# GpSimd applies the first norm's weight and bias to x; the projection weights are split as they are

## The chip, the cores and the metric

One core of one Trainium2 chip runs the kernel. The metric is device time in microseconds (us); times of before are the median of three runs. Lower is better.

## The reference

Two attention layers run one after the other over 32 sequences of 128 tokens with 512 features, all in float32. What matters here, with one layer's names (layer 0 has 16 heads and ordinary softmax attention, layer 1 has 8 heads and linear attention with one softmax over the head's features for q and one over the tokens for k):

```python
xn = layer_norm(x) * norm_w + norm_b          # first norm, over 512 features
q, k, v = xn @ q_w + q_b, xn @ k_w + k_b, (xn @ v_w + v_b) * mask
y = attention(q, k, v)
e = silu(cond) @ emb_w + emb_b; scale, shift = split(e)
h = (layer_norm(y) * w2 + b2) * (1 + scale) + shift      # second norm
x = x + silu(h) @ out_w + out_b
```

## The kernel before

**Stages.** Sequences go in pairs (GROUP = 2); G = 16 pairs per layer, so there are 32 pair-steps in all, 0 to 15 for layer 0 and 16 to 31 for layer 1. In one step three pairs are in work at once: `k` (attention, second norm and output), `f` = the next pair (projections q, k, v) and `n` = the one after (load, first norm, transposition to `xt`). `late` is the second sequence of the pair before `k`, whose output is finished in this step. Sequences of a pair are slots b = 0 and 1. The step of pair 15 is `step_mixed`: attention of layer 0 beside projections of layer 1. Steps 0, 13, 14, 15, 16 and the last three are written out; the others run in two loops.

**Engines.** Each engine has its own list of work in a fixed order, written by hand in `start`, `step0`, `step_mixed` and `step1`, and waits on semaphores. No planner moves anything. All DMAs are issued by SyncE (SP), in order.
- TensorE (PE): each projection is computed as three float32r products, high times high, low times high and high times low (`three`, L1276 to L1278). Transpositions of xn (`turn`, L1272) and of yn (`turn_yn`, L1368) are matmuls with the identity.
- VectorE (DVE): moments of the norms (L880, L884), low parts (`w_lo` L835, `xt_lo` L893, `s_lo` L954), softmax pieces, `film_scale` (L941), silu (L948), output (L960).
- ScalarE (ACT): exponentials, tanh (L632), high parts (`w_hi` L570 and L572, `xt_hi` L584, `s_hi` L637), copies out of PSUM.
- GpSimd (POOL): finishes both norms. `rsqrt_norm` does three one-column operations (L454, L455, L457) and one over 128x512 (L462), which reads x_in and writes xn in `norm1`, or reads y_s and writes yn in `norm2`. It also adds the output bias to the residual (`residual`, L493), masks v (`v_mask`, L478 and L482) and adds the shift (`add_shift`, L488, writes z_s).

**GpSimd's order in a step of layer 1** (`step1`): norm1(n,0), residual(k,0), norm2(k,0), norm1(n,1), v_mask(f,0), norm2(k,1), add_shift(k,0), add_shift(k,1), v_mask(f,1), residual(k,1). In layer 0 (`step0`): norm1(n,0), residual(k,0), norm1(n,1), norm2(k,0), residual(k,1), v_mask(f,0), add_shift(k,0), norm2(k,1), v_mask(f,1), add_shift(k,1).

**TensorE's order in a step of layer 1**, from the middle on: query(k,0) (L1417), the first half of the values, query(k,1), queries1(f,0), turn_yn(k,0), values(f,1), turn_yn(k,1), queries1(f,1), turn(n,0), output(k,0), turn(n,1), then of the next step the transpositions of k and q, output(late,1), keys and again query.

**The norm's weight and bias before.** The first norm's w is folded into the weights: `high_part` and `low_part` scale each weight chunk by a column of w (`col[:, l, NW]`) as they split it. The norm's bias is folded into the projections' biases: for each of six weights (`TURN` lists them) `bias_part` (L1231, eight matmuls) multiplies norm_b with the raw weight into four row groups, ScalarE copies the result out (`bias_part_out`, L580), `bias_sum` (L1242 or L1245) adds the groups up on TensorE, and VectorE adds the sum to the bias (`bias_col` L844, `bias_wide` L849). Three of the six stand in `start`, one in step 13, one in step 14 and one in `step_mixed`.

```python
a = raw[l][j][c // 2][:, c % 2]
act.activation(hi[l][j][:, c], a, ACT.Identity, scale=col[:, l, NW, c:c + 1])
```

Of the kernel before, what the change touches and what calls it, by code (L numbers as in the profile page):

```python
# [7 lines left out]
BF16 = mybir.dt.bfloat16  # L8
# [47 lines left out]
def build(nc, t, out):  # L56
# [27 lines left out]
    with ExitStack() as ctx:  # L84
# [6 lines left out]
        def chunks(ap):  # L91
# [16 lines left out]
        col = sb("col", [P, 2, 6, C])  # L108
        NW, NBI, W2, B2, QB, KB = range(6)
        wide = sb("bias_wide", [P, 5, D])  # L110
        VALUE_BIAS, OUT_BIAS, QUERY_BIAS = (0, 3), (1, 4), 2
        film_ab = sb("film_ab", [P, 2, 2, C, B])
        silu_cond = film_ab[:, 1].rearrange("p i c b -> p (i c b)").rearrange("p (k b) -> p k b", k=KE)
        mask_parts = sb("mask_parts", [B, 3, P], BF16)
# [6 lines left out]
        ones_32nd = sb("ones_32nd", [P, P])  # L121
        norm_b_32 = sb("norm_b_32", [P, C, 32])
# [13 lines left out]
        y_t = sb("y_t", [P, D])  # L136
        y_s = sb("y_s", [P, D])
# [63 lines left out]
        PARS = (16 * 8, 16 * 6)  # L201
# [4 lines left out]
        spread, bias_pe, bias_act, bias_sum_pe, bias_dve = (  # L206
            sem(n) for n in ("spread", "bias_pe", "bias_act", "bias_sum_pe", "bias_dve"))
        TURN = {(0, WQ): 1, (0, WK): 2, (0, WV): 3, (1, WK): 4, (1, WV): 5, (1, WQ): 6}
        bias_part_at = [None, spare, y_t, spare, spare, spare, spare]
# [11 lines left out]
        s = stages("stats aggr rstd_a rstd_b neg_mean xn_full xn_turned xt_high xt_low "  # L221
# [56 lines left out]
        def _(sp):  # L278
# [10 lines left out]
            def load_wide(l, j, row):  # L289
                sp.dma_start(wide[:, row, :], layers[l]["b"][j].rearrange("(o n) -> o n", o=1).broadcast_to([P, D])  # L290
                             ).then_inc(par_in[l], 16)
# [41 lines left out]
            def start():  # L333
# [4 lines left out]
                load_wide(0, WV, VALUE_BIAS[0])  # L338
                load_col(0, QB, WQ, par_in[0])
# [5 lines left out]
                load_col(0, KB, WK, par_in[0])  # L345
                load_wide(0, WO, OUT_BIAS[0])
# [5 lines left out]
                for j in (WQ, WK):  # L352
                    sp.wait_ge(bias_pe, TURN[0, j])
                    sp.wait_ge(w_split[0][j], 1)
                    load_emb(0, (4 + 2 * j, 5 + 2 * j))
# [7 lines left out]
                load_wide(1, WQ, QUERY_BIAS)  # L363
                load_wide(1, WV, VALUE_BIAS[1])
                load_wide(1, WO, OUT_BIAS[1])
# [5 lines left out]
                sp.wait_ge(bias_sum_pe, 3)  # L371
                load_emb_bias(1, eb1_in)

            def step0(i, n, f, k, late, slot):
# [21 lines left out]
                if i == G - 2:  # L396
                    sp.wait_ge(bias_pe, TURN[1, WK])
                    sp.wait_ge(w_split[1][WK], 1)
                    load_weight(1, WQ)

            def step_mixed(i, n, f, k, late, slot):
                load_front(1, n)
                load_back(0, k, 0)
                store(0, late, 1)
                load_back(0, k, 1)
                sp.wait_ge(*done(s["pv"], LAST0))
                load_weight(1, WO)
                store(0, k, 0)
# [26 lines left out]
        def _(pool):  # L435
# [5 lines left out]
            pool.memset(ones_32nd[:], 1.0 / 32).then_inc(once, 1)  # L441
            pool.memset(ones_parts[:], 0.0).then_inc(once, 1)
            pool.wait_ge(once, 5)
# [3 lines left out]
            pool.wait_ge(once, 6)  # L447
            pool.tensor_tensor(pick[:], ident[:, 0:2 * B], ident[:, 2 * B:4 * B], ALU.add).then_inc(consts, 1)

            def rsqrt_norm(b, which, mv, a_in, rs, nm, full, src_ap, dst_ap, at, dst_free):  # L450
# [11 lines left out]
                pool.tensor_scalar(dst_ap, src_ap, v[:, 10:11], v[:, 9:10], ALU.add, ALU.mult  # L462
                                   ).then_inc(s[full].sem, 1)

            def norm1(n, b):
                pool.wait_ge(*landed(s["x_in_full"], n, b))
                rsqrt_norm(b, 0, "aggr", "rstd_a", "rstd_b", "neg_mean", "xn_full",
                           x_in[:, b, :], xn[:, b, :], n + b, "xn_turned")

            def norm2(k, b):  # L470
                rsqrt_norm(b, 1, "aggr2", "rstd2_a", "rstd2_b", "neg_mean2", "yn_full",
                           y_s[:], yn[:, b, :], k + b, "h_pe")
# [23 lines left out]
            def start():  # L496
                for b in range(GROUP):
                    norm1(pair(0), b)
                pool.memset(mask_wide[:], 0.0).then_inc(wide_clear, 1)
                for b in range(GROUP):  # L500
                    norm1(pair(1), b)
# [4 lines left out]
            def step0(i, n, f, k, late, slot):  # L506
                norm1(n, 0)
# [3 lines left out]
                norm1(n, 1)  # L511
# [15 lines left out]
            def step1(i, n, f, k, late, slot):  # L527
                if n:
                    norm1(n, 0)
                if i == G:  # L530
                    pool.wait_ge(par_in[1], PARS[1])
                    pool.wait_ge(film_dve, 6)
# [3 lines left out]
                if n:  # L536
                    norm1(n, 1)
# [21 lines left out]
        def _(act):  # L559
            act.wait_ge(consts, 1)  # L560

            def high_part(l, j, some=range(C)):
                act.wait_ge(w_in[l][j], 32)
                act.wait_ge(norm_in[l], 16 * 2)
# [10 lines left out]
            def bias_part_out(l, j, b):  # L575
                n = TURN[l, j]
                act.wait_ge(bias_pe, n)
                if n > 2:
                    act.wait_ge(bias_sum_pe, n - 2 if n == 3 else n - 1)
                act.activation(bias_part_at[n][:], bank[b][:], ACT.Copy).then_inc(bias_act, 1)  # L580
# [82 lines left out]
            def start():  # L663
# [5 lines left out]
                bias_part_out(0, WQ, 2)  # L669
                high_part(0, WK)  # L670
                act.wait_ge(bias_dve, 1)
                q_out(f, 0, 0)
                bias_part_out(0, WK, 3)
# [4 lines left out]
                bias_part_out(0, WV, 2)  # L678
                high_part(0, WO)
                act.wait_ge(bias_dve, 2)  # L680
# [5 lines left out]
            def step0(i, n, f, k, late, slot):  # L686
# [18 lines left out]
                if i == G - 3:  # L705
                    bias_part_out(1, WK, 6)
# [7 lines left out]
                if i == G - 2:  # L714
                    bias_part_out(1, WV, 6)
# [12 lines left out]
            def step_mixed(i, n, f, k, late, slot):  # L728
# [4 lines left out]
                act.wait_ge(bias_dve, TURN[1, WK])  # L733
# [10 lines left out]
                bias_part_out(1, WQ, 1)  # L744
# [60 lines left out]
        def _(dve):  # L805
            dve.wait_ge(consts, 1)

            def spread_norm_b(l):
                dve.wait_ge(norm_in[l], 16 * 2)
                dve.tensor_copy(norm_b_32[:], col[:, l, NBI, :].rearrange("p (c o) -> p c o", o=1).broadcast_to([P, C, 32])  # L810
                                ).then_inc(spread, 1)

# [27 lines left out]

            def bias_col(l, j, i, b):
                dve.wait_ge(par_in[l], PARS[l])
                dve.wait_ge(bias_sum_pe, TURN[l, j])
                dve.tensor_tensor(col[:, l, i, :], col[:, l, i, :], bank[b][:, 0:C], ALU.add).then_inc(bias_dve, 1)  # L844

            def bias_wide(l, j, row, b):
                dve.wait_ge(par_in[l], PARS[l])
                dve.wait_ge(bias_sum_pe, TURN[l, j])
                dve.tensor_tensor(wide[:, row, :], wide[:, row, :], bank[b][:], ALU.add).then_inc(bias_dve, 1)  # L849
# [162 lines left out]
            def start():  # L1012
# [3 lines left out]
                spread_norm_b(0)  # L1016
# [5 lines left out]
                bias_col(0, WQ, QB, 5)  # L1022
# [7 lines left out]
                bias_col(0, WK, KB, 5)  # L1030
# [6 lines left out]
                bias_wide(0, WV, VALUE_BIAS[0], 5)  # L1037
                dve.wait_ge(bias_dve, TURN[0, WV])
# [7 lines left out]
            def step0(i, n, f, k, late, slot):  # L1046
                if late:
                    film_scale(0, late + (-1), 1)
                if i == G - 3:
                    spread_norm_b(1)  # L1050
# [23 lines left out]
                if i == G - 3:  # L1074
                    bias_col(1, WK, KB, 6)
# [6 lines left out]
                if i == G - 2:  # L1082
                    bias_wide(1, WV, VALUE_BIAS[1], 3)
# [12 lines left out]
            def step_mixed(i, n, f, k, late, slot):  # L1096
# [16 lines left out]
                dve.wait_ge(bias_dve, TURN[1, WV])  # L1113
# [9 lines left out]
                bias_wide(1, WQ, QUERY_BIAS, 4)  # L1123
                dve.wait_ge(bias_dve, TURN[1, WQ])
# [78 lines left out]
        def _(pe):  # L1203
# [20 lines left out]

            def bias_part(l, j, b):

                claim(b, times(bias_act, TURN[l, j]))
                pe.wait_ge(spread, l + 1)
                pe.wait_ge(w_in[l][j], 32)
                for c in range(C):  # L1230
                    last = pe.matmul(bank[b][32 * c:32 * (c + 1), :], norm_b_32[:, c, :], raw[l][j][c // 2][:, c % 2],  # L1231
                                     start=True, stop=True, tile_position=(0, 32 * c))
                last.then_inc(bias_pe, 1)

            def bias_sum(l, j, b, as_column):
                n = TURN[l, j]
                claim(b, times(bias_dve, n))
                pe.wait_ge(bias_act, n)
                part = bias_part_at[n]
                if as_column:  # L1240
                    for c in range(C):
                        last = pe.matmul(bank[b][:, c:c + 1], part[:, c * P:(c + 1) * P], ones_32nd[:, 0:1],  # L1242
                                         start=True, stop=True)
                else:
# [355 lines left out]
```

## Time and profile before

| | |
|---|---|
| median of 3 runs | 1098.57 us (1097.37 to 1098.67) |
| the profiled execution's own time | 1097.78 us |
| its span, first to last instruction | 1096.0 us |
| mean granted TensorE clock | 0.993 |
| TensorE matmul busy | 1054.8 us, 96% |
| VectorE, ScalarE, GpSimd busy | 759.8, 591.6, 448.6 us |

The profile is of one execution. Busy time is that of instructions, without waits; matmuls overlap, so a busy TensorE need not be at its peak. The granted clock is the share of full speed, 2.4 GHz, that TensorE had; 0.5 is 1.2 GHz.

### The profile page before, as it was taken

Reading aid. Unit: us, or ns where it says so; the run is one execution under the profiler, and the core shown is the slowest. Engines: PE = TensorE matmul, PEld = TensorE weight load, DVE = VectorE, ACT = ScalarE, POOL = GpSimd, SP = SyncE. Lnnn points to the kernel's source line nnn. Section 1 sums busy time; section 2 is a strip of 40 time slices with the busy share of each in tenths; the row PEclk is TensorE's granted clock in tenths of the full one; section 3 lists DMA queues with packets and bytes.
Section 4 is the critical chain, followed back from the end, with each engine's and each line's share of the span. In section 5 each row is a group of like instructions: output and inputs, shape, how many; then the busy total and the mean of one; then the engine's idle time right before and its main releaser. Section 6 shows DMA issues by size and latency. Waiting matters only on the chain. (4 is left out here: it accounts for less than half of the span.)

```text
span 1096.0 us, 25953 instructions
## 1 busy us (share of the span) xinstructions
PE 1054.8 (96%) x8696; PEld 909.8 (83%) x8696; DVE 759.8 (69%) x1326; ACT 591.6 (54%) x1960; POOL 448.6 (41%) x783
## 2 busy tenths in 40 slices
PE   6999999999999999999999999999999999999995
PEld 4878888888888888888887778888888888888884
DVE  4656766676666766667678787777777777777764
ACT  5366667776677766776588443433343443434431
POOL 3242434334343343433343344444444444444432
PEclk9999999999999999999999999999999999999997
DMA  8824110111101111011102211111111111111011
GB/s 275 256 84 141 42 61 24 62 62 41 60 24 62 62 41 59 25 62 63 43 23 98 95 50 33 40 55 57 57 57 57 57 57 57 52 52 39 31 38 58
DMA packets 46017, 71.65 MB, mean 65 GB/s; under 512 B 10256, under 2 KB 14448, under 8 KB 45968
## 3 DMA queue, kind: packets, MB, share of 16 engines
q1 hardware_dynamic: 45968, 71.02, 20.3%
q8 instruction: 27, 0.44, 0.2%
q14 instruction: 22, 0.18, 0.1%
HBM read 54.19 MB, written 16.79 MB: 65 GB/s over the span
## 5 line engine op out<-in xcount | busy, mean ns | idle before, releaser
L1276 PE MATMUL bank<-xt_hi,w_hi 128*128 128x256 f32 x768 | 228.4, 297 | 3.1 <-DVE xt_lo L893 3.1
L1277 PE MATMUL bank<-xt_lo,w_hi 128*128 128x256 f32 x768 | 218.5, 284 | 0.0
L1278 PE MATMUL bank<-xt_hi,w_lo 128*128 128x256 f32 x768 | 218.3, 284 | 0.0
L454 POOL TENSOR_SCALAR stat<-stat 128x1 f32<-128x1 f32 x128 | 34.5, 270 | 441.8 <-DVE stat L884 417.7
L613 ACT ACTIVATE prob<-prob,neg_max 128x128 f32<-128x128 f32 x512 | 198.7, 396 | 6.7 <-DVE neg_max L907 6.6
L632 ACT ACTIVATE th<-z_s 128x512 f32<-128x512 f32 x64 | 40.5, 633 | 249.9 <-POOL z_s L488 249.8
L1276 PE MATMUL bank<-w_hi,xt_hi 128*128 128x512 f32 x384 | 158.3, 412 | 1.0 <-DVE w_lo L835 1.0
L1276 PEld LDWEIGHTS bank<-xt_hi,w_hi 128*128 128x128 f32 x768 | 148.9, 194 | 9.1 <-DVE w_lo L835 4.8
L1278 PE MATMUL bank<-w_hi,xt_lo 128*128 128x512 f32 x384 | 150.5, 392 | 0.0
L1277 PE MATMUL bank<-w_lo,xt_hi 128*128 128x512 f32 x384 | 149.8, 390 | 0.0
L1277 PEld LDWEIGHTS bank<-xt_lo,w_hi 128*128 128x128 f32 x768 | 148.6, 193 | 0.0
L1278 PEld LDWEIGHTS bank<-xt_hi,w_lo 128*128 128x128 f32 x768 | 148.2, 193 | 0.0
L1276 PE MATMUL bank<-w_hi,s_hi 128*128 128x512 f32 x256 | 106.7, 417 | 7.2 <-DVE s_lo L954 5.1
L488 POOL TENSOR_TENSOR z_s<-z_a,film_ab 128x512 f32<-128x512 f32 x64 | 68.5, 1071 | 107.2 <-DVE z_a L941 103.3
L1278 PE MATMUL bank<-w_hi,s_lo 128*128 128x512 f32 x256 | 101.1, 395 | 0.0
L1277 PE MATMUL bank<-w_lo,s_hi 128*128 128x512 f32 x256 | 100.5, 393 | 0.0
L613 ACT ACTIVATION_READ_ACCUMULATOR prob<-prob,neg_max 128x1 f32 x512 | 99.7, 195 | 0.0
L904 DVE TENSOR_TENSOR prob<-bank,mask_row 128x512 f32<-128x512 f32 x128 | 87.6, 684 | 12.7 <-PE bank L1327 12.1
L493 POOL TENSOR_TENSOR x_res<-x_res,bias_wide 128x512 f32<-128x512 f32 x64 | 88.7, 1386 | 16.2 <-DMA x_res<-between_layers 16.2
L621 ACT ACTIVATE room<-bank 128x512 f32<-128x512 f32 x128 | 74.4, 593 | 31.5 <-PE bank L1338 29.6
L907 DVE TENSOR_REDUCE neg_max<-prob 128x4 f32<-128x512 f32 x128 | 87.9, 687 | 4.4
L948 DVE SCALAR_TENSOR_TENSOR th<-th,z_s 128x512 f32<-128x512 f32 x64 | 47.2, 737 | 62.4 <-ACT th L632 61.4
(130 smaller groups left out, 2203.3 us busy)
## 6 DMA issues: line engine op xcount, KB each, us to landing
x_in<-in_x_dram SPq DMA_DIRECT2D x32, 256.0 KB, 2.8
x_res<-in_x_dram SPq DMA_DIRECT2D x32, 256.0 KB, 2.9
between_layers<-x_res SPq DMA_DIRECT2D x32, 256.0 KB, 2.0
x_in<-between_layers SPq DMA_DIRECT2D x32, 256.0 KB, 2.8
x_res<-between_layers SPq DMA_DIRECT2D x32, 256.0 KB, 2.8
out_dram<-x_res SPq DMA_DIRECT2D x32, 256.0 KB, 2.6
room<-in_L_cond_W_emb_dram SPq DMA_DIRECT2D x8, 512.0 KB, 7.3
prob<-in_L_cond_emb_w_dram SPq DMA_DIRECT2D x4, 512.0 KB, 7.5
```

What stands on the lines that cost most here:

```text
L454: pool.tensor_scalar(v[:, 8:9], v[:, 7:8], EPS, None, ALU.add).then_inc(s[a_in].sem, 1)
L488: pool.tensor_tensor(chunks(z_s[:, b, :]), chunks(z_a[:]), film_of(l, 1, k + b), ALU.add).then_inc(s["z_full"].sem, 1)
L493: pool.tensor_tensor(x_res[:, b, :], x_res[:, b, :], wide[:, OUT_BIAS[l], :], ALU.add).then_inc(s["res_full"].sem, 1)
L613: last = act.activation(prob[:, b, i, :], prob[:, b, i, :], ACT.Exp, bias=neg_max[:, b, i:i + 1], accum_out=row_sum[:, b, h:h + 1])
L621: act.activation(prob_t[:, g, :], bank[FIRST["PT"][g % 2]][:], ACT.Copy).then_inc(s[f"pt_out{g}"].sem, 1)
L632: act.activation(th[:], z_s[:, b, :], ACT.Tanh, scale=0.5).then_inc(s["tanh_full"].sem, 1)
L904: dve.tensor_tensor(prob[:, b, heads, :], bank[c][:].rearrange("p (r n) -> p r n", r=HC0), row, ALU.add).then_inc(s[f"masked{c}"].sem, 1)
L907: dve.tensor_reduce(neg_max[:, b, heads], prob[:, b, heads, :], AX.X, ALU.max, negate=True).then_inc(s[f"neg{c}"].sem, 1)
L948: dve.scalar_tensor_tensor(out=s_s[:], in0=th[:], scalar=1.0, in1=z_s[:, b, :], op0=ALU.add, op1=ALU.mult).then_inc(s["s_full"].sem, 1)
L1276: pe.matmul(o, a_hi, b_hi, start=start, stop=False)
L1277: pe.matmul(o, a_hi, b_lo, start=False, stop=False)
L1278: return pe.matmul(o, a_lo, b_hi, start=False, stop=stop)
```

## The change

`col` loses the norm's two columns; instead `wide`, rows spread over all 128 partitions, gets two rows per layer (`NORM_ROWS`) with w and b of the first norm. GpSimd multiplies w into xn and adds b, in two more operations behind the old one, each waiting for the one in front by a semaphore. The weights are split without the scale, and `bias_part`, `bias_part_out`, `bias_sum`, `bias_col`, `bias_wide` and `spread_norm_b` are gone with all their calls. SyncE loads 128x512 rows instead of columns in `load_norm`; two bias rows of layer 1 are loaded in step 14 and one in `step_mixed`, when rows come free. `mask_parts` moves into `y_t`, so ScalarE waits once, in step 0, for its transfer.

```diff
+            def load_row(v, row, signal):
+                sp.dma_start(wide[:, row, :], v.rearrange("(o n) -> o n", o=1).broadcast_to([P, D])).then_inc(signal, 16)
             def load_norm(l):
-                load_col(l, NBI, "nb", norm_in[l])
-                load_col(l, NW, "nw", norm_in[l])
+                load_row(layers[l]["nw"], NORM_ROWS[l][0], norm_in[l])
+                load_row(layers[l]["nb"], NORM_ROWS[l][1], norm_in[l])
...
                 if i == G - 2:
-                    sp.wait_ge(bias_pe, TURN[1, WK])
+                    sp.wait_ge(*done(s["xn_full"], LAST0))
+                    load_wide(1, WV, VALUE_BIAS[1], late_in)
+                    load_wide(1, WQ, QUERY_BIAS, late_in)
                     sp.wait_ge(w_split[1][WK], 1)
...
-                pool.tensor_scalar(dst_ap, src_ap, v[:, 10:11], v[:, 9:10], ALU.add, ALU.mult
-                                   ).then_inc(s[full].sem, 1)
+                return v[:, 10:11], v[:, 9:10]
-            def norm1(n, b):
+            def norm1(l, n, b):
                 pool.wait_ge(*landed(s["x_in_full"], n, b))
+                mean, scale = rsqrt(b, 0, "aggr", "rstd_a", "rstd_b", "neg_mean", n + b, "xn_turned")
+                w, bias = (wide[:, row, :] for row in NORM_ROWS[l])
+                row = xn[:, b, :]
+                pool.tensor_scalar(row, x_in[:, b, :], mean, scale, ALU.add, ALU.mult).then_inc(s["xn_centred"].sem, 1)
+                pool.wait_ge(*done(s["xn_centred"], n + b))
+                pool.tensor_tensor(row, row, w, ALU.mult).then_inc(s["xn_scaled"].sem, 1)
+                pool.wait_ge(*done(s["xn_scaled"], n + b))
+                pool.tensor_tensor(row, row, bias, ALU.add).then_inc(s["xn_full"].sem, 1)
...
             def start():
+                pool.wait_ge(norm_in[0], 16 * 2)
                 for b in range(GROUP):
-                    norm1(pair(0), b)
+                    norm1(0, pair(0), b)
...
-                    if j == WO:
-                        act.activation(hi[l][j][:, c], a, ACT.Copy, scale=0.5).then_inc(w_high[l][j], 1)
-                    else:
-                        act.activation(hi[l][j][:, c], a, ACT.Identity, scale=col[:, l, NW, c:c + 1]
-                                       ).then_inc(w_high[l][j], 1)
+                    act.activation(hi[l][j][:, c], a, ACT.Copy, scale=0.5 if j == WO else 1.0).then_inc(w_high[l][j], 1)
...
-                                                    scalar=0.5 if j == WO else col[:, l, NW, c:c + 1],
+                                                    scalar=0.5 if j == WO else 1.0,
...
-                bias_part(0, WQ, 2)
                 need(0, WQ)
                 queries0(f, 0, 0)
-                bias_sum(0, WQ, 5, True)
-                bias_part(0, WK, 3)
                 queries0(f, 0, 1)
```

## Rows read from the trace of the kernel before

**Rows 1.** The page: busy time of the engines.
```profile
PE 1054.8 (96%) x8696; PEld 909.8 (83%) x8696; DVE 759.8 (69%) x1326; ACT 591.6 (54%) x1960; POOL 448.6 (41%) x783
```

**Rows 2.** Waits from 660 to 1040 us: who for whom, us, times, longest.
```profile
ACT th L632 <- POOL z_s L488: 107.1, 26, 5.7
PE bank L1276 <- DVE s_lo L954: 0.6, 4, 0.2
```

**Rows 3.** Layer-1 step, GpSimd in order of time: start, length, [idle before].
```profile
895.16 0.23 POOL L454 TENSOR_SCALAR stat<-stat 128x1 f32<-128x1 f32 x1 [8.19 <-DVE stat L884]
897.19 1.29 POOL L493 TENSOR_TENSOR x_res<-x_res,bias_wide 128x512 f32<-128x512 f32 x1
900.86 0.23 POOL L454 TENSOR_SCALAR stat<-stat 128x1 f32<-128x1 f32 x1 [2.39 <-DVE stat L884]
903.29 0.23 POOL L454 TENSOR_SCALAR stat<-stat 128x1 f32<-128x1 f32 x1 [0.39 <-DVE stat L884]
904.56 0.77 POOL L462 TENSOR_SCALAR xn<-x_in,stat 128x512 f32<-128x512 f32 x1 [0.21 <-POOL stat L457]
905.67 0.70 POOL L482 TENSOR_SCALAR v_s<-v_s,mask_now 128x512 f32<-128x512 f32 x1 [0.20 <-DVE stat L884]
907.73 0.77 POOL L462 TENSOR_SCALAR yn<-y_s,stat 128x512 f32<-128x512 f32 x1 [0.21 <-POOL stat L457]
908.47 1.05 POOL L488 TENSOR_TENSOR z_s<-z_a,film_ab 128x512 f32<-128x512 f32 x1
915.15 1.71 POOL L493 TENSOR_TENSOR x_res<-x_res,bias_wide 128x512 f32<-128x512 f32 x1
```

**Rows 4.** The same step on TensorE: turn_yn(k,1), and output(late,1) of the next step.
```profile
909.17 0.60 PE L1368 MATMUL bank<-ident,yn 128*128 128x128 f32 x4
917.55 0.47 PE L1276 MATMUL bank<-w_hi,s_hi 128*128 128x512 f32 x1
```

**Rows 5.** The same step on VectorE, where it is near GpSimd's chain.
```profile
898.97 0.69 DVE L932 TENSOR_TENSOR y_s<-bank,q_rec 128x512 f32<-128x512 f32 x1 [2.44 <-PE bank L1417]
908.75 1.32 DVE L988 TENSOR_TENSOR room<-spare,q_max 128x512 f32<-128x512 f32 x1
910.22 0.69 DVE L948 SCALAR_TENSOR_TENSOR th<-th,z_s 128x512 f32<-128x512 f32 x1 [0.15 <-ACT th L632]
918.03 0.69 DVE L988 TENSOR_TENSOR room<-spare,q_max 128x512 f32<-128x512 f32 x1
```

**Rows 6.** The end of the kernel: a matmul of TensorE behind a long idle time.
```profile
1084.84 0.77 PE L1276 MATMUL bank<-w_hi,s_hi 128*128 128x512 f32 x1 [3.16 <-DVE s_lo L954]
```

**Rows 7.** Windows, TensorE: stretch, length, busy (instructions), granted clock, DMA share, GB/s.
```profile
1084.80:1089.60 4.80, 4.65 (x12) 0.63 0.01 2
917.50:920.40 2.90, 2.85 (x13) 1.00 0.00 0
```

**Rows 8.** Layer-0 step: GpSimd's norm2(k,0), and TensorE's turn_yn(k,0).
```profile
453.33 0.23 POOL L454 TENSOR_SCALAR stat<-stat 128x1 f32<-128x1 f32 x1 [2.08 <-DVE stat L884]
457.62 0.60 PE L1368 MATMUL bank<-ident,yn 128*128 128x128 f32 x4
```

**Rows 9.** The mixed step (15) and the first step of layer 1 (16).
```profile
597.31 0.23 POOL L454 TENSOR_SCALAR stat<-stat 128x1 f32<-128x1 f32 x1 [1.30 <-DVE stat L884]
599.50 0.63 PE L1368 MATMUL bank<-ident,yn 128*128 128x128 f32 x4
...
638.96 0.63 PE L1368 MATMUL bank<-ident,yn 128*128 128x128 f32 x4 [0.39 <-POOL yn L462]
```

**Rows 10.** The start: GpSimd's second xn, TensorE's first projection, two groups of bias matmuls.
```profile
8.10 0.77 POOL L462 TENSOR_SCALAR xn<-x_in,stat 128x512 f32<-128x512 f32 x1 [0.21 <-POOL stat L457]
...
15.02 0.55 PE L1276 MATMUL bank<-xt_hi,w_hi 128*128 128x256 f32 x1 [3.11 <-DVE xt_lo L893]
21.05 1.06 PE L1231 MATMUL bank<-room,norm_b 128*32 128x512 f32 x8
565.83 1.12 PE L1245 MATMUL bank<-spare,ones_32nd 128*128 128x512 f32 x2
```

More of the change, by code:

```diff
@@ L106, in build @@
         lo = [{j: w_lo[:, p] for j, p in place[l].items()} for l in range(2)]
[L108 to L111, printed above, removed]
+        col = sb("col", [P, 2, 4, C])
+        W2, B2, QB, KB = range(4)
+        wide = sb("wide", [P, 6, D])
+        VALUE_BIAS, OUT_BIAS, QUERY_BIAS, NORM_ROWS = (0, 3), (1, 0), 2, ((2, 3), (4, 5))
         film_ab = sb("film_ab", [P, 2, 2, C, B])
         silu_cond = film_ab[:, 1].rearrange("p i c b -> p (i c b)").rearrange("p (k b) -> p k b", k=KE)
-        mask_parts = sb("mask_parts", [B, 3, P], BF16)
         mask_row = sb("mask_row", [P, GROUP, P])
@@ L205, in build @@
         EMB_SUMS = (2, 4, 5)
[L206 to L209, printed above, removed]
+        qk_in, late_in, out_in = (sem(n) for n in ("qk_in", "late_in", "out_in"))
         w_in = [[sem(f"w_in{l}{j}") for j in range(4)] for l in range(2)]
@@ L405, in step_mixed @@
                 load_back(0, k, 1)
+                sp.wait_ge(*done(s["v_add"], LAST0))
+                load_wide(1, WO, OUT_BIAS[1], out_in)
                 sp.wait_ge(*done(s["pv"], LAST0))
@@ L446, in _, with rsqrt @@
             last.then_inc(once, 1)
-            pool.wait_ge(once, 6)
+            pool.wait_ge(once, 5)
             pool.tensor_tensor(pick[:], ident[:, 0:2 * B], ident[:, 2 * B:4 * B], ALU.add).then_inc(consts, 1)
-            def rsqrt_norm(b, which, mv, a_in, rs, nm, full, src_ap, dst_ap, at, dst_free):
+            def rsqrt(b, which, mv, a_in, rs, nm, at, dst_free):
                 v = stat[:, which, b, :]
@@ L506, in step0 @@
             def step0(i, n, f, k, late, slot):
-                norm1(n, 0)
+                if i == G - 2:
+                    pool.wait_ge(norm_in[1], 16 * 2)
+                norm1(1 if i in (G - 2, G - 1) else 0, n, 0)
                 if i == 0:
@@ L510, in step0 @@
                 residual(0, k, 0)
-                norm1(n, 1)
+                norm1(1 if i in (G - 2, G - 1) else 0, n, 1)
                 norm2(k, 0)
@@ L528, in step1 @@
                 if n:
[L529 removed]
+                    norm1(1, n, 0)
                 if i == G:
[L531 removed]
+                    pool.wait_ge(out_in, 16)
                     pool.wait_ge(film_dve, 6)
@@ L536, in step1 @@
                 if n:
-                    norm1(n, 1)
+                    norm1(1, n, 1)
                 if f:
@@ L1223, in need @@
                 pe.wait_ge(w_split[l][j], 1)
[L1225 to L1244, printed above, removed]
-                    last = pe.matmul(bank[b][:], ones_32nd[:], part[:], start=True, stop=True)
-                last.then_inc(bias_sum_pe, 1)
             def embed(l, some, b, sums):
@@ L1435, in start @@
                 last.then_inc(mask_pe, 1)
-                bias_part(0, WV, 2)
                 need(0, WK)
                 keys(0, f, 0, 0)
-                bias_sum(0, WK, 5, True)
                 keys(0, f, 0, 1)
@@ L1447, in start @@
                 values(0, FIRST, f, 0, 0)
-                bias_sum(0, WV, 5, False)
                 values(0, FIRST, f, 0, 1)
@@ L1467, in step0 @@
                 keys(0, f, slot, 0)
-                if i == G - 3:
-                    bias_part(1, WK, 6)
                 weigh(k, 1 - slot, 0)
@@ L1472, in step0 @@
                 y_rows(k, 0)
-                if i == G - 2:
-                    bias_part(1, WV, 6)
                 keys(0, f, slot, 1)
@@ L1483, in step0 @@
                 weigh(k, 1 - slot, 1)
-                if i == G - 2:
-                    bias_sum(1, WV, 3, False)
                 turn(n, 0)
@@ L1510, in step_mixed @@
                 values(1, MIXED, f, slot, 0)
-                bias_part(1, WQ, 1)
                 weigh(k, 1 - slot, 0)
@@ L1518, in step_mixed @@
                 weigh(k, 1 - slot, 1)
-                bias_sum(1, WQ, 4, False)
                 turn(n, 0)
```

88 lines of the change are left out of this document (20 added, 68 removed).

## The prediction

> **What bounds the kernel now.** I read the page first: TensorE is busy for 96% of the span, GpSimd for 41% [rows 1]. By shares alone GpSimd has more than half of its time free, and taking matmuls off TensorE should pay. Shares are averages, though, so next the waits of the uniform part of layer 1, 660 to 1040 us [rows 2]: TensorE waits there for almost nothing, but ScalarE's tanh waits 107 us for GpSimd's z_s. GpSimd stands in a chain, and the question is how late it may be. TensorE waits only 0.6 us in all for s_lo, with which that chain ends.
>
> Third, one step of that part in order of time (its period is 29.9 us). VectorE begins with y of slot 0 as soon as TensorE's query is through, having idled 2.44 us for it [rows 5]; from there to turn_yn(k,1) nothing waits for TensorE except the products it makes itself. GpSimd starts norm2(k,0) at 900.86 and norm1(n,1) at 903.29; its wide operation is over at 905.33; v_mask is issued behind it and runs at 905.67; norm2(k,1) ends with yn at 908.50; z_s(k,0) comes at 908.47 to 909.52 [rows 3]. TensorE takes that yn at 909.17 [rows 4]: the slack is 0.66 us. Silu(k,0) on VectorE waited 0.15 us for z_s by way of tanh [rows 5], and the same chain releases output(late,1) at 917.55 just in time [rows 2, 4]. So in layer 1 the loop TensorE query, VectorE, GpSimd, TensorE is already as long as TensorE's work.
>
> **The added work, in a layer-1 step.** xn gets two more 128x512 operations. The row of the same form, x_res plus a wide row in place, takes 1.29 us undisturbed [rows 3]. A GpSimd operation that waits for the one in front begins 0.20 us after it (0.21 before L462, 0.20 before L482) [rows 3]. That makes 2 x (1.28 + 0.20) = 2.96 us per sequence. Bounds: 1.05 us, the z_s form, gives 2.50; 1.71 us, the disturbed form, gives 3.82 [rows 3]. I take 1.28, the identical form.
>
> By the Trainium skill's GPSIMD Engine Reference (section "Elementwise — side-by-side cycle accounting") a two-input operation costs about 2.6 cycles per element; my estimate from it is 1.11 us for 512 elements at 1.2 GHz. It would make the term 2.6 instead of 2.96 and the forecast some 4 us lower.
>
> *norm1(n,1)* stands ahead of v_mask, norm2(k,1) and add_shift(k,0) in GpSimd's list, so all three are 2.96 us late. *norm1(n,0)* begins at 895.16; with its extra 2.96 and the residual, GpSimd is free at 901.45 instead of 898.48, and norm2(k,0), which could start at 900.86, loses 0.6 us; the 0.39 us idle before norm1(n,1) takes most of that back [rows 3]. In every second step norm1(n,0) begins some 0.4 us later against the query. I take 0.3 for both. Third, v_mask would now start at about 908.8, beside VectorE's L988 at 908.75. That instruction took 0.69 us alone and 1.32 us beside z_s, and x_res took 1.71 instead of 1.29 us beside VectorE's work [rows 3, 5]: the two engines hold each other up. Here v_mask waits 0 to 0.6 us, I take 0.3. Sum: 3.56 us.
>
> The Trainium skill's SBUF — State Buffer (section "SBUF: two separate sides") says why: VectorE instructions with two SBUF inputs and GpSimd's share one port pair under an exclusive lock, and the later one waits for the whole of the other. The rows agree in sign and size.
>
> Out of 3.56, about 0.15 is slack at the silu, and nothing at output(late,1). **3.4 us per step.** norm1 with a tail behind it runs in steps 17 to 29: 13 x 3.4 = 44.2 us.
>
> **The clock.** TensorE now stands idle some 3 us at turn_yn(k,1). In this trace such idle times occur only at the end: after 3.16 us the matmul at 1084.84 took 0.77 us against 0.47 for its like [rows 4, 6]. The twelve matmuls of that output had a mean granted clock of 0.63, between the levels 1.2 and 2.4 GHz, and were busy 4.65 us against 2.85 for one in the loop [rows 7]: 1.8 us for one drop. Some of a drop falls on the idle time itself; 0.4 us is covered, since output(late,1) waits 3.4 us longer for s_lo but turn_yn only 3.0; and not each stall need bring one. I take 0.8 per step, 10.4 us; bounds 0 and 1.4.
>
> **Layer 0.** GpSimd's norm1(n,1) ended 2.08 us before norm2(k,0) began; 2.96 makes norm2 0.9 us late. With the 2.05 us from its first operation to its last, yn was ready at 455.4, and TensorE takes it at 457.62, 2.2 us later [rows 8]. It is hidden in steps 1 to 14, and so is norm1(n,0), with over 3 us free behind it. If that cover went, each us would cost some 14.
>
> **Steps 15 and 16.** In the mixed step the idle before norm2(k,0) was 1.30, so it starts 1.66 late, and TensorE had taken yn just as it came [rows 9]: +1.6. In step 16 TensorE already waits 0.39 us for yn [rows 9], and low parts of a weight run beside GpSimd: +3.2.
>
> **The removed work.** A bias_part is 1.06 us of TensorE, a wide bias_sum 1.12 [rows 10], each about 0.1 less in pitch, the column sum about 0.85. In steps 13 and 14, where TensorE is full: -3.8. The group in step 15 lies in waits: 0. The instructions taken from ScalarE (six copies) and VectorE (six additions, two spreads) lie beside TensorE's work: 0 each. The unscaled split gains nothing for the same reason.
>
> **The start.** Before the first projection (15.02) TensorE waited 3.11 us, for xt_lo; GpSimd's second xn was ready at 8.87 [rows 10]. Now four more operations (5.9 us) and the wait for the two spread rows (about 1 us) put it at 16 or 17, and xt of slot 1, behind turn and two splits of about 0.6 us, at 19 to 20: +4.5. Two bias_parts and three bias_sums after 15.02 go away: -4.6. Net 0, bounds -4 and +4. SyncE issues two wide rows (512 KB) ahead of the first weight; they take the place of two slow column loads, and the later norms hide them. SyncE's new waits in steps 14 and 15 are for stages done a step before; behind them stand weight loads with a step of room: 0. ScalarE's wait for the mask transfer in step 0: 0.
>
> **Sum.** 44.2 + 10.4 + 1.6 + 3.2 - 3.8 = 55.6 us on the profiled execution's 1097.78 us (0.8 below the median of the runs): 1153.4.
>
> **The rivals.**
> - *The clock stays up* (27%): idle 3 us in a 33 us step is no idle kernel; but the only comparable rows speak against it. 1097.8 + 45.2 = 1143; with the 1.05 us price 1130.
> - *More mutual blocking* (10%): both operations at 1.71, and VectorE's silu and s_lo held too. 0.84 us and some clock more per step: 1165 to 1180. For it: rows 3 and 5. Against: in the old order the slots of the new operations meet no VectorE instruction with two SBUF inputs.
> - *Partly absorbed* (7%): the step closes up after the stall and pays under 2.5 us: 1112 to 1130.
> - *Hidden, and faster* (5%): at turn_yn(k,1) the lateness stays within the 0.66 us of slack. Above that point each step pays. GpSimd spans are rough, so operations might overlap; then only removals show, 3.8 and up to 4 at the start: 1090 to 1094. The 0.20 us gaps before dependent operations speak against it.
> - *The change does no harm or good* (1%): a balance by chance.
>
> **Numbers.** The forecast has 50%, 1144 to 1164 by itself. The range 1130 to 1172 takes in the case without a clock drop and the milder half of blocking. About 0.2% is what a measurement of this kernel can tell from no change. Slower 0.93, same 0.02, faster 0.05.
>
> **What would show it.** GpSimd: two new groups of 64 operations, 1.25 to 1.5 us each, busy time near 615 us. Layer-1 steps 33 to 34.5 us apart, layer-0 steps still 34.4. TensorE: a wait for yn of 2.5 to 3.3 us before turn_yn(k,1) in steps 17 to 29, and below it a granted clock under 1.0 in layer 1. The forecast is wrong if that wait is under 1 us, if another engine ends it, or if layer-0 steps grow.

## The result and the profile after

| | before | after |
|---|---|---|
| median (5 runs each) | 1098.57 us (1096.48 to 1098.69) | 1153.88 us (1151.72 to 1158.62) |
| profiled execution, its span | 1097.78, 1096.0 us | 1158.62, 1156.6 us |
| its mean granted clock | 0.993 | 0.970 |

The changed kernel is slower: ratio 1.051, 95% interval 1.0485 to 1.0534, against a forecast of 1153.4. The profiled execution is the longest of its five, 4.7 us above the median; steps counted in its trace come out a little too long.

The page of the changed kernel, busy time of the engines; it answers to [rows 1]:

```profile
PE 1059.4 (92%) x8618; PEld 913.2 (79%) x8618; DVE 751.4 (65%) x1318; ACT 586.0 (51%) x1954; POOL 620.4 (54%) x910
```

TensorE has 78 matmuls fewer and is busy 4.6 us longer; I put that down to the lower clock, and no run separates it. GpSimd went from 448.6 to 620.4 us. Its two new groups, from the view of instructions by line (busy, mean ns | idle before):

```profile
L469 POOL TENSOR_TENSOR xn<-xn,wide 128x512 f32<-128x512 f32 x64 | 82.8, 1294 | 5.0
L467 POOL TENSOR_TENSOR xn<-xn,wide 128x512 f32<-128x512 f32 x64 | 82.7, 1293 | 5.3
```

Price (1.29 us) and count are as forecast. The idle in front is 5.0 and 5.3 us over 64, 0.08 us each, not 0.20.

The waits of the uniform part, 700 to 1090 us (total, times, longest), which answer to [rows 2]:

```profile
ACT th L624 <- POOL z_s L489: 137.7, 23, 9.7
...
DVE th L919 <- ACT th L624: 69.3, 23, 4.8
...
PE bank L1305 <- POOL yn L473: 33.4, 12, 3.4
```

In each of these steps TensorE now waits 2.8 us for yn on the mean; in the kernel before no step from 17 to 29 has such a wait. Each engine behind z_s is late too. TensorE's turn_yn(k,1) in order of time, steps 16, 17, 23, 24 and 29, the number in brackets is the idle time in front:

```profile
644.83 0.63 PE L1305 MATMUL bank<-ident,yn 128*128 128x128 f32 x4 [3.54 <-POOL yn L473]
...
678.95 0.63 PE L1305 MATMUL bank<-ident,yn 128*128 128x128 f32 x4 [2.87 <-POOL yn L473]
...
883.01 0.63 PE L1305 MATMUL bank<-ident,yn 128*128 128x128 f32 x4 [2.35 <-POOL yn L473]
...
916.88 0.63 PE L1305 MATMUL bank<-ident,yn 128*128 128x128 f32 x4 [3.44 <-POOL yn L473]
...
1086.69 1.08 PE L1305 MATMUL bank<-ident,yn 128*128 128x128 f32 x4 [2.89 <-POOL yn L473]
```

The same instruction of step 29 in the kernel before:

```profile
1028.78 0.60 PE L1368 MATMUL bank<-ident,yn 128*128 128x128 f32 x4
```

From step 16 to 29 that is (1086.69 - 644.83) / 13 = 33.99 us a step, against (1028.78 - 638.96) / 13 = 29.99 before (638.96 in [rows 9]): 4.00 us more, 52.0 in all. After minus before, the trace stands at +2.5 us at turn_yn(k,0) of the mixed step (602.02 against 599.50), +5.9 at step 16, +57.9 at step 29 and +60.6 at the end of the span. TensorE in the mixed step of after:

```profile
602.02 1.09 PE L1305 MATMUL bank<-ident,yn 128*128 128x128 f32 x4 [4.84 <-POOL yn L473]
```

GpSimd in one layer-1 step of after, in order of time; it answers to [rows 3]:

```profile
909.52 0.78 POOL L465 TENSOR_SCALAR xn<-x_in,stat 128x512 f32<-128x512 f32 x1 [0.21 <-POOL stat L453]
910.38 1.29 POOL L467 TENSOR_TENSOR xn<-xn,wide 128x512 f32<-128x512 f32 x1
911.75 1.30 POOL L469 TENSOR_TENSOR xn<-xn,wide 128x512 f32<-128x512 f32 x1
912.99 0.71 POOL L479 COPY mask_now<-mask_col 128x1 f32 x1
913.90 0.69 POOL L483 TENSOR_SCALAR v_s<-v_s,mask_now 128x512 f32<-128x512 f32 x1 [0.21 <-POOL mask_now L479]
...
915.96 0.77 POOL L473 TENSOR_SCALAR yn<-y_s,stat 128x512 f32<-128x512 f32 x1 [0.21 <-POOL stat L453]
916.70 1.05 POOL L489 TENSOR_TENSOR z_s<-z_a,film_ab 128x512 f32<-128x512 f32 x1
```

The reader sees the forecast's mechanism: v_mask, norm2(k,1) and add_shift stand behind the two new operations. L479, one column, took 0.71 us where it mostly takes 0.18 or 0.19; VectorE's L959 began 0.03 us before it and ended 0.05 us before it:

```profile
912.96 0.69 DVE L959 TENSOR_TENSOR room<-spare,q_max 128x512 f32<-128x512 f32 x1
```

The clock of TensorE, in windows of after behind turn_yn(k,1) of steps 22 (848.53, idle 3.44) and 23 (883.01, idle 2.35); columns: window, length, then busy us and count of PE, PEld, DVE, ACT, POOL, then the granted clock:

```profile
850.00:852.00 2.00, 2.00 (x7) 1.52 (x6) 1.80 (x3) 1.22 (x3) 0.00 (x0) 0.50 0.00 0
...
885.00:887.00 2.00, 2.00 (x12) 1.53 (x11) 1.90 (x4) 0.69 (x2) 0.00 (x0) 1.00 0.00 0
```

After one stall of this kind TensorE ran at 1.2 GHz for a while, after the other at 2.4 GHz. The clock dropped in 7 of the 13 steps 17 to 29, and in 15 and 16.

### The profile page after: what moved, and what is told of

The parts are those of the page before. It is cut to its first block and busy times, and to the rows that moved or that the text cites. A ratio compares the mean times of both kernels' runs of the same rounds, so it can differ in the third digit from the quotient of the medians.

```text
span 1156.6 us, 25881 instructions
## 1 busy us (share of the span) xinstructions
PE 1059.4 (92%) x8618; PEld 913.2 (79%) x8618; DVE 751.4 (65%) x1318; ACT 586.0 (51%) x1954; POOL 620.4 (54%) x910
## 5 line engine op out<-in xcount | busy, mean ns | idle before, releaser
L450 POOL TENSOR_SCALAR stat<-stat 128x1 f32<-128x1 f32 x128 | 37.1, 290 | 344.1 <-DVE stat L855 313.1
L1214 PE MATMUL bank<-xt_lo,w_hi 128*128 128x256 f32 x768 | 216.1, 281 | 0.0
L1213 PE MATMUL bank<-w_hi,xt_hi 128*128 128x512 f32 x384 | 164.7, 429 | 1.4 <-DVE prob L875 1.4
L1215 PE MATMUL bank<-w_hi,xt_lo 128*128 128x512 f32 x384 | 157.3, 410 | 0.0
L1214 PE MATMUL bank<-w_lo,xt_hi 128*128 128x512 f32 x384 | 156.8, 408 | 0.0
L494 POOL TENSOR_TENSOR x_res<-x_res,wide 128x512 f32<-128x512 f32 x64 | 88.8, 1388 | 17.9 <-DMA x_res<-between_layers 17.9
L1215 PEld LDWEIGHTS bank<-w_hi,xt_lo 128*128 128x128 f32 x384 | 76.0, 198 | 17.5
```

The source lines that it names most:

```text
L450: pool.tensor_scalar(v[:, 8:9], v[:, 7:8], EPS, None, ALU.add).then_inc(s[a_in].sem, 1)
L494: pool.tensor_tensor(x_res[:, b, :], x_res[:, b, :], wide[:, OUT_BIAS[l], :], ALU.add).then_inc(s["res_full"].sem, 1)
L1213: pe.matmul(o, a_hi, b_hi, start=start, stop=False)
L1214: pe.matmul(o, a_hi, b_lo, start=False, stop=False)
L1215: return pe.matmul(o, a_lo, b_hi, start=False, stop=stop)
```

## The experiments

In the kernels e1 to e4 a part of the first norm is left out: both row operations (weight and bias) in e1, those of layer 1 in e2, those of layer 0 in e3, the bias in e4. The other kernels compute everything. Ratios are to the kernel before, runs on the same chip.

### How much of it is the row operations, and where

e1 leaves both out:

```diff
-                pool.tensor_scalar(row, x_in[:, b, :], mean, scale, ...).then_inc(s["xn_centred"].sem, 1)
-                pool.wait_ge(*done(s["xn_centred"], n + b))
-                pool.tensor_tensor(row, row, w, ALU.mult).then_inc(s["xn_scaled"].sem, 1)
-                pool.wait_ge(*done(s["xn_scaled"], n + b))
-                pool.tensor_tensor(row, row, bias, ALU.add).then_inc(s["xn_full"].sem, 1)
+                pool.tensor_scalar(row, x_in[:, b, :], mean, scale, ...).then_inc(s["xn_full"].sem, 1)
```

> The kernel after without GpSimd's two new operations in either layer (the norm's weight and bias are left out of xn; loads and all else stay). Theory, that the loss is GpSimd's lateness: layer-1 steps go back to 29.9 us, and with the removed TensorE work (-3.8) the time is 1092 to 1098. Rival, that the loss comes from the moved loads or other waits: above 1110.

Measured 1086.8 us, ratio 0.9913 (0.9893 to 0.9933). So the row operations cost 1153.9 - 1086.8 = 67 us, and all the rest of the change gives 10 back (1097.03 of the kernel before on the same chip, less 1086.8): the forecast counted 8.4 for the removed work (3.8 in steps 13 and 14, 4.6 at the start).

Not all of the 10 is removed work, though. TensorE's products with 256 columns became shorter. One of their three lines in before, after and e1 (busy, mean ns | idle before):

```profile
L1278 PE MATMUL bank<-xt_hi,w_lo 128*128 128x256 f32 x768 | 218.3, 284 | 0.0
L1215 PE MATMUL bank<-xt_hi,w_lo 128*128 128x256 f32 x768 | 216.0, 281 | 0.0
L1211 PE MATMUL bank<-xt_hi,w_lo 128*128 128x256 f32 x768 | 214.2, 279 | 0.0
```

From turn_yn(k,0) of step 2 to that of step 12 a layer-0 step takes 34.43 us before, 34.17 in after and 33.93 in e1, with the same number of matmuls; in the changed kernel and all twelve variants it is 33.90 to 34.17. The forecast kept these steps at 34.4. Why the products became shorter no run shows.

e2 keeps them in layer 0 alone, e3 in layer 1 alone (`if l == 0:` or `if l == 1:` around them).

> The two operations only for pairs of layer 0 (left out for layer 1). Theory: layer-0 steps hide them, only the start pays, 1096 to 1104, layer-0 steps 34.4 us. Rival, that GpSimd's added load disturbs VectorE wherever it runs: half of the loss stays, 1120 or more.

> The two operations only for pairs of layer 1 (left out for layer 0). Theory: nearly the whole loss stays, 1145 to 1154. Rival: 1125 or less.

e2: 1095.18 us, 0.9981 (0.997 to 0.9992), 8.4 over e1. e3: 1144.25 us, 1.0431 (1.0414 to 1.0448), 57.5 over e1. The two add up to 65.9 of the 67. The 8.4 arise at the start: at turn_yn(k,0) of step 1 the trace of e2 is 9.2 us behind that of e1 (118.20 against 108.99), at step 12 still only 9.7. The start of before (GpSimd's first operation of the norm) and of after (GpSimd, TensorE, and SyncE's DMA queue), for [rows 10]:

```profile
4.70 0.23 POOL L454 TENSOR_SCALAR stat<-stat 128x1 f32<-128x1 f32 x1 [1.76 <-DVE stat L884]
```
```profile
9.23 0.23 POOL L450 TENSOR_SCALAR stat<-stat 128x1 f32<-128x1 f32 x1 [6.43 <-DMA wide<-in_L_cond_norm_b_dram]
```
```profile
20.09 1.11 PE L1209 MATMUL bank<-ident,xn 128*128 128x128 f32 x4 [4.89 <-POOL xn L469]
22.71 0.55 PE L1213 MATMUL bank<-xt_hi,w_hi 128*128 128x256 f32 x1 [1.51 <-DVE xt_lo L864]
...
46.05 0.63 PE L1209 MATMUL bank<-ident,xn 128*128 128x128 f32 x4 [2.58 <-POOL xn L469]
```
```profile
13.99 6.41 SPq L314 DMA_DIRECT2D x_in<-in_x_dram  x2
20.45 0.42 SPq L342 DMA_DIRECT2D z_a<-in_mask_BxS_ff_dram  x1
```

GpSimd waits for the norm's bias row before any of the norm; the first projection is at 22.71 instead of 15.02, 7.7 us late and not 4.5. At 46.05 TensorE waits once more for GpSimd, 2.58 us for xn of pair 1, which it did not do before.

e4 keeps the multiply and leaves the bias out.

> Only the multiplication, in both layers (the bias is left out). Theory: one operation makes GpSimd 1.36 us late per sequence, the slack of 0.66 us at turn_yn leaves TensorE an idle time under 1 us, so the step grows by about 1.2 us and the clock stays up: 1108 to 1119, which is under half of the loss. Rival, without threshold and clock, cost in proportion to the operations: 1124 to 1128.

Measured 1110.94 us, 1.0128 (1.0111 to 1.0145). From none to one operation 24.1 us, from one to two 42.9. Half the work costs 36% of the time. TensorE's wait for yn, 700 to 1050 us, in e4:

```profile
PE bank L1303 <- POOL yn L471: 10.5, 11, 1.0
```

1.0 us a step, against 2.8 with both, and a granted clock of 0.993: the slack and the clock make the cost bent, as the theory had it. By the numbers, 13 x 0.66 us of slack and the 7.4 us of e6 below are 16 of the 18.8 us between the two halves; the rest was not traced.

### What the clock costs

e6 is the changed kernel with 20 transpositions of `ident` on TensorE ahead of turn_yn(k,1), whose result nobody reads:

```diff
                 claim(to, (s["z_a_full"], k + b))
+                for _ in range(fill):
+                    pe.transpose(bank[to][:, 0:P], ident[:], ident[:])
```

> The kernel after with twenty transpositions of the identity on TensorE ahead of turn_yn(k,1) in steps 16 to 29, where it stood idle; their output is written over. The wait for yn stays where it is. Theory with a clock share: granted clock 1.0 in those steps, 6 to 12 us less, 1142 to 1148. Rival, that the clock drops cost nothing because the chain through s_lo ends later: 1152 to 1156.

Measured 1146.48 us, 1.0449 (1.0431 to 1.0467): with useless work it is 7.4 us faster, at a granted clock of 0.992. Waits of 700 to 1090 us and the window 660 to 1080:

```profile
PE bank L1307 <- POOL yn L473: 8.3, 12, 1.4
```
```profile
660.00:1080.00 420.00, 405.66 (x2804) 348.15 (x2802) 274.07 (x489) 143.66 (x406) 244.46 (x357) 1.00 0.15 46
```

Most of the idle time is filled (0.7 us a step is left), the lateness stays, and the clock does not drop. So the clock's share of the change is about 7 us (6.7 by the ratios), and the rest is lateness.

### SyncE's order

e7 issues layer 1's two wide bias rows behind x_in in the mixed step instead of ahead of Wq in step 14:

```diff
                 if i == G - 2:
-                    sp.wait_ge(*done(s["xn_full"], LAST0))
-                    load_wide(1, WV, VALUE_BIAS[1], late_in)
-                    load_wide(1, WQ, QUERY_BIAS, late_in)
...
             def step_mixed(i, n, f, k, late, slot):
                 load_front(1, n)
+                sp.wait_ge(*done(s["xn_full"], LAST0))
+                load_wide(1, WV, VALUE_BIAS[1], late_in)
+                load_wide(1, WQ, QUERY_BIAS, late_in)
```

The reason was a row of after, VectorE in the mixed step:

```profile
585.81 0.70 DVE L851 BATCH_NORM_STATS2 stat<-x_in 128x6 f32<-128x512 f32 x1 [4.25 <-DMA x_in<-between_layers]
```

> The kernel after with layer 1's two bias rows issued behind x_in of the mixed step and not ahead of the weight and of x_in. Theory: VectorE's 4.25 us wait for x_in goes, yn in the mixed step comes earlier: 2 to 3 us less, 1150 to 1152. Rival, that GpSimd ends that wait anyway: 1153 to 1155.

Measured 1149.85 us (1146.57 to 1152.37), 1.0475 (1.045 to 1.0501): 4.0 us under after, with ranges that just overlap. The trace settles it; TensorE in the mixed step of e7:

```profile
597.56 0.63 PE L1305 MATMUL bank<-ident,yn 128*128 128x128 f32 x4 [2.38 <-POOL yn L473]
```

From turn_yn(k,0) of step 14 to this one it is 36.3 us, against 40.5 in after and 35.7 before.

e8 moves x_in of pair 1 behind the output weight at the start, so that nothing is queued behind its wait.

> The kernel after with x_in of pair 1 loaded behind the output weight in SyncE's list, so that its wait for GpSimd's first norms no longer holds up masks, biases and weights. Theory: most of what the start loses is GpSimd's norms themselves, 0 to 2 us less, 1151 to 1154. Rival, that SyncE's blocked list is the start's loss: 3 to 5 us less.

Measured 1154.81 us, 1.0533 (1.0515 to 1.0552): no gain. In its trace GpSimd still waits for the bias row (to 8.25 us), TensorE's first projection is at 21.72 and its wait for xn of pair 1 2.27 us. So what is queued behind x_in's wait is not what the start loses.

### Another place for the same work

e5 moves norm1(n,1) behind add_shift(k,0) in `step1`:

```diff
-                if n:
-                    norm1(1, n, 1)
                 if f:
                     v_mask(f, slot, 0)
                 if k:
                     norm2(k, 1)
                     add_shift(1, k, 0)
+                if n:
+                    norm1(1, n, 1)
+                if k:
                     add_shift(1, k, 1)
```

> The kernel after with both operations, but in layer-1 steps norm1(n,1) moves on GpSimd behind add_shift(k,0), so it is no longer ahead of v_mask(f,0), norm2(k,1) and add_shift(k,0). Theory: yn of slot 1 is in time again, the step returns to 29.9 to 30.8 us (add_shift(k,1) may be up to 0.9 us late): 1098 to 1112. Rival, that GpSimd's load as such costs, whatever the order: over 1140.

Measured 1134.3 us, 1.0336 (1.0319 to 1.0353), between both expectations. TensorE no longer waits for yn, but a new wait took its place. GpSimd, VectorE and TensorE of e5, in order of time:

```profile
903.43 1.23 POOL L465 TENSOR_SCALAR xn<-x_in,stat 128x512 f32<-128x512 f32 x1 [0.21 <-POOL stat L453]
...
907.37 1.05 POOL L489 TENSOR_TENSOR z_s<-z_a,film_ab 128x512 f32<-128x512 f32 x1
```
```profile
909.12 0.86 DVE L920 SCALAR_TENSOR_TENSOR th<-th,z_s 128x512 f32<-128x512 f32 x1 [4.39 <-ACT th L625]
```
```profile
910.63 0.66 PE L1325 MATMUL bank<-ident,q_t 128*128 128x128 f32 x4 [1.49 <-DVE spare L951]
911.80 0.77 PE L1214 MATMUL bank<-w_hi,s_hi 128*128 128x512 f32 x1 [0.51 <-DVE s_lo L926]
```

norm1(n,1) took 6.1 us there (901.32 to 907.4, its operation over x_in 1.23 instead of 0.78 beside VectorE's work), and the gap between the two add_shift is 3.6 us. z_s(k,1) comes late, silu(k,1) waits 4.39 us, and q_add stands behind silu on VectorE, so TensorE waits for both.

e11 puts into that gap only what fits, the centring, and the rows behind add_shift(k,1). turn(n,1) with xt_high and xt_low moves into the next step:

```diff
                     add_shift(1, k, 0)
+                if n:
+                    centre(n, 1)
+                if k:
                     add_shift(1, k, 1)
+                if n:
+                    rows(1, n, 1)
...
                     turn_k(k, 1 - slot, 1)
+                if f and i != G:
+                    turn(f, 1)
```

> From layer 1's steps 16 on, the row operations of slot 1 get a place where nothing that decides waits for them: norm1(n,1) is only centred between add_shift(k,0) and add_shift(k,1), where GpSimd waited 3.57 us for z_a; its multiply and add follow add_shift(k,1), and turn(n,1) with xt_high and xt_low of slot 1 moves into the next step, behind turn_k(k,1). Theory (what layer 1 lost was the two places, turn_yn(k,1) and then add_shift(k,1), and not the work as such): the steps come back to 29.9 to 30.3 us, turn_yn(k,1) and silu(k,1) wait for nothing new, the granted clock stays above 0.99; the layer-1 share of the 57 us goes but for 0 to 6, so 1096 to 1104 us. Rival (GpSimd and VectorE get in each other's way on the memory, so the 5.4 us of row operations per step cost wherever they stand): steps of 31 us or more, over 1112 us.

Measured 1136.91 us, 1.0372 (1.0358 to 1.0386): a miss. turn_yn does not wait and silu at most 1.8 us, as before the change, but TensorE of e11 stands elsewhere, for VectorE, which waited for ScalarE:

```profile
915.33 0.28 PE L1240 MATMUL bank<-mask_wide,ones_parts 128*128 x1 [1.99 <-DVE xt_lo L875]
```
```profile
911.50 0.63 ACT L653 ACTIVATE room<-room 128x512 f32<-128x512 f32 x1 [2.05 <-DVE room L970]
912.03 0.58 ACT L658 ACTIVATE prob<-bank 128x512 f32<-128x512 f32 x1
912.52 0.59 ACT L663 ACTIVATE prob<-bank 128x512 f32<-128x512 f32 x1
912.99 0.60 ACT L658 ACTIVATE prob<-bank 128x512 f32<-128x512 f32 x1
913.47 0.61 ACT L586 ACTIVATE xt_hi<-bank 128x512 fp32r<-128x512 f32 x1
```

I had moved xt_high behind q_exps and three copies. TensorE turned xn of slot 1 at 909.97, yet xt_high ran at 913.47, and keys waited for it.

e12 adds e7's order and a start in which both slots are centred before GpSimd waits for the norm's rows; x_in's next load waits for the centring only.

```diff
+                for b in range(GROUP):
+                    centre(pair(0), b)
                 pool.wait_ge(norm_in[0], 16 * 2)
                 for b in range(GROUP):
-                    norm1(0, pair(0), b)
+                    rows(0, pair(0), b)
```

> As e11_late, and two more places: at the start both slots of pair 0 are centred before GpSimd waits for the norm's rows (they landed at 9.2 us, the statistics at 5.2), x_in's next load waits for the centring instead of the whole norm, and in the mixed step the two wide bias rows are issued behind x_in. Theory: the start gives back 4 to 6 of the 8.4 us that the rows cost there (two centrings and their small operations, 2 x 2.0 us, and the 2.1 us by which slot 1's were stretched), the mixed step 2 to 3: 1089 to 1097 us, below the kernel before. Rival (the weights' loads and not the norm set the first projection): only the mixed step's 2 to 3 us under e11_late.

Measured 1129.0 us, 1.0289 (1.0275 to 1.0303), 7.9 under e11. The absolute forecast missed with e11's; the start did not. TensorE's first projection in e12:

```profile
18.09 0.55 PE L1228 MATMUL bank<-xt_hi,w_hi 128*128 128x256 f32 x1 [2.53 <-DVE xt_lo L877]
```

4.6 us earlier than in after.

e13 is e12 with turn(n,1) behind turn_q(k,0) instead of turn_k(k,1), and xt_high and xt_low in their old places.

> e12_all with one thing moved: turn(n,1) only as far as behind turn_q(k,0) of the next step, where slot 1's xn is just ready (in e11_late GpSimd finished it at 909.44 us and TensorE would stand there at 909.53), and ScalarE's xt_high and VectorE's xt_low of slot 1 stay in their old places, ahead of q_exps and of the output. In e11_late xt_low of slot 1 came at 914.44 us because xt_high stood behind q_exps, kt_out, qt_out and kt_out, and keys waited for it up to 2.4 us with TensorE's clock down for the next 1 to 2 us. Theory: those go and with them 2.1 to 2.9 us of each of the 12 to 13 steps: 1129 - 27 to 37 = 1092 to 1102 us, granted clock 0.99. Rival (another chain sets the step as well, VectorE's around silu(k,1) and q_sub, held up by GpSimd on the memory): steps of 31 us, 1106 to 1118 us.

Measured **1090.55 us** (1087.5 to 1091.89), ratio 0.9932 (0.9919 to 0.9946). This beats both kernels and has all of the change in it. TensorE is busy again without gaps; windows of e13 and its turn_yn(k,1) of steps 17 and 30:

```profile
740.00:780.00 40.00, 39.95 (x279) 34.45 (x278) 28.72 (x53) 16.10 (x51) 29.12 (x42) 1.00 0.15 46
780.00:820.00 40.00, 39.93 (x263) 34.20 (x262) 30.41 (x52) 15.40 (x39) 30.27 (x39) 1.00 0.12 39
820.00:860.00 40.00, 40.00 (x295) 35.08 (x294) 29.57 (x54) 16.07 (x44) 25.41 (x35) 1.00 0.22 72
```
```profile
663.39 0.60 PE L1317 MATMUL bank<-ident,yn 128*128 128x128 f32 x4
...
1048.85 0.60 PE L1317 MATMUL bank<-ident,yn 128*128 128x128 f32 x4
```

(1048.85 - 663.39) / 13 = 29.65 us a step, with GpSimd doing all that work; in the kernel before the same 13 steps take 29.89 us each (670.03 to 1058.63). The 7 us under the kernel before are no gain from the row operations, but come with the rest of the change: e1, without them, is at 1086.8, 4 us lower still by the medians and 2 by the ratios, though its start and mixed step are those of the changed kernel.

e14 has e13's layer 1 alone, start and mixed step as in the changed kernel.

> e13_near without its two smaller parts: only layer 1's order is changed (centring of slot 1 between the two add_shift, its rows behind them, turn(n,1) behind turn_q(k,0) of the next step); start and mixed step are as in the changed kernel. Theory: the start's 5 us and the mixed step's 2 to 4 come back, 1097 to 1100 us, so the placement alone brings the change level with the kernel before and the start makes it faster. Rival (start and mixed step are absorbed later, as 3.7 us of the start's lateness was): 1091 to 1094 us.

Measured 1094.03 us (12 runs), 0.9979 (0.9969 to 0.9988), between both. The order in layer 1 alone takes 1153.88 to 1094.03, 60 us. Start and mixed step are worth 3.5 us more by the medians and 5.2 by the ratios, less than the 7.9 between e11 and e12. The two profiled executions are 7.6 us apart (spans 1093.9 and 1086.3), but each lies 2.1 us from its median, to opposite sides, so whether anything is absorbed later stays open.

## Why the prediction was right, and where not

- *What bounds layer 1, and the 0.66 us of slack*: right. The wait for yn at turn_yn(k,1) came in every step from 16 to 29 (2.33 to 3.54 us), and e5 and e13 remove it by the order alone. e3 and e2 put 57.5 us into layer 1 and 8.4 into the start.
- *The added work, 2 x (1.28 + 0.20)*: the operations are 1.29 us; the gap was mis-sized. The rows with 0.20 us are of instructions behind a `nop`; a directly dependent operation of the new chain began 0.08 us after the one in front (910.38 + 1.29 to 911.75). The term is 2.7 instead of 2.96.
- *3.4 us a step and 0.8 for the clock*: 4.2 forecast, 4.0 measured in the profiled execution. In e6 the clock is 7.4 us in all, not 10.4, and where it stays up, steps 17 to 29 are 33.4 us apart against 29.9 before: 3.5 us for the lateness, though the two operations cost 0.2 less than forecast. What makes up that difference was not traced. The even split of the clock over steps was not real: it dropped in 7 of 13.
- *The rival of more mutual blocking*: it exists, but only to the 0.3 us that the forecast gave it: in 7 of the 13 steps one of v_mask(f,0)'s two operations took 0.26 to 0.54 us longer than in the others (as L479 at 0.71), which is 0.25 us a step on the mean. It counts in e5, where the norm came to stand beside VectorE's two-input instructions.
- *The rival of a clock that stays up* (1143): e6 made it real with other means and came to 1146.5. Without fill the clock did drop. Its second figure, 1130 at a price of 1.05 us, does not come out of the forecast's own terms: 0.46 us less in 13 steps and in 15 and 16 makes 1136.
- *Layer 0 hidden*: right for the rows: steps 2 to 12 take 33.99 us each in e2 and 33.93 in e1, and e2's loss is that of the start. But the steps did not stay at 34.4: with the shorter products they take 34.17 in after, which gives 3.0 us back between steps 1 and 12, a term that the forecast does not have.
- *The start, net 0*: the step failed, by 4.3 us, just outside its bounds. I costed the wait for the two rows at about 1 us and xn of slot 1 at 16 or 17 us. The bias row let GpSimd begin at 9.23 instead of 4.70, 4.5 us later, and the second norm's operations took longer beside the weights' split on VectorE (the multiply 1.57, the add 1.59 us), so xn was ready at 20.0. The first projection was 7.7 us late, and the wait of 2.58 us at 46.05 I had not foreseen. The removed bias groups paid a part: layer 0's scores began 5.3 us late (50.17 against 44.83). The trace stood at +4.3 us at turn_yn(k,0) of step 1 (117.58 against 113.32) and, by the shorter products, at +1.3 at that of step 12 (493.33 against 492.05).
- *The removed work in steps 13 and 14, -3.8*: about right. From step 12 to step 14 the trace gains 3.5 us (to -2.2 at turn_yn(k,0) of step 14, 561.54 against 563.76); some 0.5 of it is the products again.
- *Step 15, +1.6*: the step failed, by 3.1 us; it measured +4.7, from -2.2 to +2.5. SyncE's 512 KB of bias rows ahead of x_in made the statistics wait 4.25 us, which I had costed at 0, and TensorE waited 4.84 us for yn (602.02). The mixed step (turn_yn(k,0) of step 14 to that of 15) is 4.7 us longer than before in after, 2.0 in e1 with SyncE's order but no row operations (550.43 to 588.14), and 0.6 in e7 with the operations but not that order. So the two delays add to each other, and SyncE's, which I had left out, is the larger; the row operations alone cost less than the 1.6.
- *Step 16, +3.2*: right, 3.35 measured (5.87 - 2.52).
- *The sum*: the trace of after is 60.6 us longer in its span: 2.5 up to the mixed step, 3.4 in step 16, 52.0 in steps 17 to 29, 2.7 behind them. The forecast has -2.2, 3.2, 54.6 and 0 for the same four. So it is 5.0 us short in all, and as the profiled execution is 4.7 us above its median, the median fell within 1 us. That closeness is partly luck: a start, a mixed step and an end costed too low (4.3, 3.1 and 2.7 us) against a clock share costed too high and layer-0 steps that became shorter for a reason the forecast does not have. The mechanism in layer 1 is not luck.

The Trainium skill's GPSIMD Engine Reference (section "Elementwise — side-by-side cycle accounting") gives about 2.6 cycles per element for a two-input operation. My estimate of 1.11 us from it is 0.18 us too short for the new operations: the page and the trace differ, and the measured 1.29 us decides. Where the second input is a broadcast column (z_s) the trace has 1.05 us.

## What to carry to other kernels

An engine at 41% busy can still be the one that sets the step: before you give it work, find the operation of its list that TensorE takes just as it comes, and count what stands ahead of it. Then look for a place behind the last operation that someone waits for, put in the gaps only what fits them, and move the readers of the late result on every engine, but no further than the result is ready. The same row operations cost 67 us in one order (after against e1) and 2 to 4 in another (e13 against e1).

## What the runs showed of the hardware beyond what I had expected

- One stall in each 34 us step dropped the granted clock, but not every time: of steps 17 to 29 it fell at six of the seven stalls of 2.87 to 3.44 us and at one of the six of 2.33 to 2.42. With 3.44 us once it fell (848.53) and once it did not (916.88). Twenty useless transpositions in the gap kept it at 1.00 and saved 7.4 us, though TensorE did more.
- On GpSimd the dependent row operations began 0.08 us after the one in front (5.0 us of idle over 64); with a `nop` between them it was mostly 0.20 to 0.21 us (L465, L473, L483).
- A one-column GpSimd operation beside a VectorE instruction with two SBUF inputs took as long as the latter: L479 0.71 us instead of 0.18, beside L959 with 0.69. An operation over 128x512 took 1.23 instead of 0.78 (e5, 903.43). The rule of the Trainium skill's SBUF — State Buffer (section "SBUF: two separate sides"), that the later one waits for the whole of the other, agrees with these rows.
